# The normalisers of a wave attention, moved from a block of their own into the sampling block

## What is computed

```python
wp = silu(x @ w_wave + b_wave).reshape(b, l, 3, H)
freq_avg  = (sigmoid(wp[:, :, 0]) * 15 + 1).mean(-1)
phase_avg = (tanh(wp[:, :, 1]) * 16).mean(-1)
decay_avg = (sigmoid(wp[:, :, 2]) * 9.5 + 0.5).mean(-1)
qk = einsum("blhd,d->blh", silu(x @ w_query + b_query).reshape(b, l, H, POS), key_weight)
sample_pos = centers + stride_grid * freq_avg + phase_avg        # stride_grid: -16 .. 16
valid = (sample_pos >= 0) & (sample_pos < l)
rel = abs(stride_grid) * freq_avg
env = exp(-rel / max(decay_avg, 0.1))
attn = softmax(where(valid, qk * rel * SCALE, -inf)) * env * valid
attn = attn / (attn.sum(-1) + 1e-8)
out = einsum("blhsd,blhs->blhd", x[sample_pos], attn)            # then gates, w_out, the rest
```

## Time and profile before

| | us |
|---|---|
| median of 3 runs | 1732.34 (1732.11 to 1733.88) |
| the profiled execution's own time | 1732.2 |
| its span | 1730.5 |
| busy: TensorE, VectorE, ScalarE, GpSimd | 1529.6, 1361.0, 1016.0, 189.7 |
| mean granted TensorE clock, of full | 0.958 |

### The profile page before, as it was taken

How to read it: one execution, slowest core, us unless ns; L and a number is a source line. 1 busy time by engine, 2 the same in 40 slices (tenths; PEclk the granted TensorE clock), 3 DMA queues, 4 the chain that set the end, 5 groups by cost and what they waited for, 6 DMA issues and landing times. The chain is left out here.

```text
span 1730.5 us, 32390 instructions
## 1 busy us (share of the span) xinstructions
PE 1529.6 (88%) x9990; PEld 833.1 (48%) x9990; DVE 1361.0 (79%) x2955; ACT 1016.0 (59%) x1734; POOL 189.7 (11%) x366
## 2 busy tenths in 40 slices
PE   6028999996998999999999999999999876999997
PEld 5025565554655323322333233333322675999997
DVE  4879999963677888888888888888884575777774
ACT  3159999962544677767777677767777442222221
POOL 0021211103111000000000000000000271222222
PEclk9569999997999999999999999999999987999999
DMA  3030101002685522221222122221211467565561
GB/s 103 0 86 13 42 20 42 20 25 85 218 247 202 140 59 69 68 63 51 61 68 68 48 53 68 67 63 53 58 44 44 133 228 272 207 212 202 201 202 55
DMA packets 159151, 171.30 MB, mean 99 GB/s; under 512 B 73102, under 2 KB 119183, under 8 KB 158992
## 3 DMA queue, kind: packets, MB, share of 16 engines
q1 hardware_dynamic: 153008, 155.54, 29.7%
q0 software_dynamic: 4432, 12.66, 1.9%
q10 hardware_dynamic: 1552, 1.30, 0.2%
HBM read 120.73 MB, written 49.23 MB: 98 GB/s over the span
## 5 line engine op out<-in xcount | busy, mean ns | idle before, releaser
L1386 DVE TENSOR_REDUCE at_mx<-at_pmx 128x1 f32<-128x512 f32 x980 | 620.0, 681 | 61.9 <-PE at_pmx L1452 60.9
L1373 ACT ACTIVATE at_p<-at_pst 128x512 f32<-128x512 f32 x1024 | 539.3, 601 | 218.9 <-PE at_pst L1471 207.9
L1452 PE MATMUL at_pmx<-at_k,at_q 96*128 96x512 bf16 x980 | 375.3, 383 | 1.0 <-DVE at_mx L1386 0.7
L1471 PE MATMUL at_pst<-at_q,at_k 99*128 99x512 bf16 x1024 | 351.9, 381 | 14.6 <-ACT at_p L1373 12.2
L1481 PE MATMUL at_pacc<-at_p,at_v 128*32 128x512 f32 x2048 | 272.8, 604 | 0.9 <-ACT at_p L1373 0.7
L1452 PEld LDWEIGHTS at_pmx<-at_k,at_q 96*128 96x128 bf16 x980 | 95.0, 97 | 237.2 <-DVE at_mx L1386 175.6
L539 ACT ACTIVATE ws_A<-ws_steps,par_beta,par_alpha 128x672 f32<-128x672 bf16 (+2 forms) x256 | 200.2, 856 | 4.8 <-issue 4.2
L629 DVE TENSOR_TENSOR ws_AT<-ws_pA,ws_hitT 128x768 f32<-128x768 f32 (+1 forms) x192 | 180.1, 950 | 16.4 <-PE ws_pA L688 15.4
L1471 PEld LDWEIGHTS at_pst<-at_q,at_k 99*128 99x128 bf16 x1024 | 99.2, 98 | 161.4 <-ACT at_p L1373 98.4
L688 PE MATMUL ws_pA<-ident,ws_A 128*128 128x128 f32 x1088 | 146.6, 280 | 25.9 <-ACT ws_A L539 24.5
L2011 DVE STREAM_TRANSPOSE ex_zr<-ex_row 32x64 f32<-32x64 f32 x608 | 143.2, 236 | 21.4 <-DMA ex_row<-scratch_routed 13.6
(11 more groups left out here) (243 smaller groups left out, 1464.0 us busy)
## 6 DMA issues: line engine op xcount, KB each, us to landing
ex_w<-in_L_ffn_w SPq DMA_DIRECT2D x39, 1024.0 KB, 5.1
at_q<-scratch_qs SPq DMA_DIRECT2D x192, 64.0 KB, 2.7
at_k<-scratch_ks SPq DMA_DIRECT2D x192, 64.0 KB, 2.8
ex_row<-scratch_routed SPq DMA_DIRECT2D x39, 258.0 KB, 4.9
scratch_v<-gp_v SPq DMA_DIRECT2D x8, 1024.0 KB, 7.8
at_v<-scratch_v SPq DMA_DIRECT2D x32, 256.0 KB, 3.3
w<-in_L_ffn_w SPq DMA_DIRECT2D x16, 512.0 KB, 4.2
scratch_qs<-gp_split SPq DMA_DIRECT2D x16, 384.0 KB, 3.1
```

What stands on the lines that cost most here:

```text
L1373: a.activation(pt[k // 2 % 4][:, k % 2, :], pst[bank(k)][:], ACT.Exp).then_inc(exped, 1)
L1386: v.reduce_max(mx[u % 2][:, m // 2, m % 2:m % 2 + 1], pmx[bank(m)][:], AX.X).then_inc(red, 1)
L1452: nc.tensor.matmul(pmx[bank(m)][:], qst[u][0:ROWS, h, nt * P:(nt + 1) * P], kst[u][0:ROWS, h, kh * HALF:(kh + 1) * HALF], start=True, stop ...
L1471: nc.tensor.matmul(pst[bank(k)][:], kst[u][:, h, t * P:(t + 1) * P], qst[u][:, h, p * HALF:(p + 1) * HALF], start=True, stop=True).then_in ...
```

## The change

The normalisers' block goes. `tanhs` and `qk` now lie in the memory of `ws_A`, which is free until the first weights, and so does a new table `spread`: it has a column for each of 64 lanes (head and tile) and each distance k from 1 to 16, and as a matmul's moving side it gives the lane's slope times k minus the lane's top. GpSimd makes it, and the iotas, in the projection block. VectorE starts the sampling block with the short chain, with counts in bf16 and 100 for 1000 as the far constant. The arguments come from TensorE: it turns slopes and tops (four groups of 64 lanes) and multiplies them with `spread`, 2 x 512 columns a group. ScalarE takes the exponentials from PSUM in four groups, with distance 0 apart. VectorE forms `share` = (env + 1e-8) x count once and weighs each group with it (min with 1, then multiply), written with the distance outermost; TensorE sums the 17 distances of a group by matmuls with the identity. Between the groups stand the first unit's tile chains. The scratch memory is that of `ws_AT`. Parts that only rename are left out of the diff.

```diff
+WINDOWS = 17 * P + 4 * 2 * 16
...
-            wave_parameters(nc, sem, sb, ps, io, dr, ident, par)
-            wave_sampling(nc, sem, sb, ps, io, dr, ident, identb, par, gate_loads, gates_in)
+            weights = sb(wave, "ws_A", [P, WH // 2, WINDOWS])
+            grid = Grid(lambda *a: sb(wave, *a), weights)
+            with ExitStack() as ctx:
+                project_waves(nc, sem, lambda *a: sb(ctx, *a), lambda *a: ps(ctx, *a), io, ident, par["lpos"], grid)
+            wave_sampling(nc, sem, sb, ps, io, dr, ident, identb, par, weights, grid, gate_loads, gates_in)
...
+class Grid:
+    NK = REACH + 1
+    FAR = 100
+    def __init__(self, sb, weights):
+        words = weights[:].rearrange("p h n -> p (h n)")
+        self.steps = sb("grid_steps", [P, STEPS])
+        self.ks = sb("grid_ks", [P, self.NK], BF16)
+        self.far = sb("grid_far", [P, self.NK], BF16)
+        self.spread = words[:, 0:1024].rearrange("p (n k) -> p n k", k=REACH)
+        self.tanhs = words[:, 1024:1792].rearrange("p (t n h) -> p t n h", n=3, h=WH)
+        self.qk = words[:, 1792:2048].rearrange("p (t h) -> p t h", h=WH)
...
+        @block.gpsimd
+        def _(pool):
+            g = nc.gpsimd
+            near = ident[:, 0:2 * TILES].unsqueeze(2).to_broadcast([P, 2 * TILES, REACH])
+            away = ident[:, 2 * TILES:P].unsqueeze(2).to_broadcast([P, 2 * TILES, REACH])
+            g.iota(grid.spread, pattern=[[0, 2 * TILES], [1, REACH]], base=1, channel_multiplier=0,
+                   allow_small_or_imprecise_dtypes=True).then_inc(made, 1)
+            g.iota(lpos[:], pattern=[[0, B], [P, BT]], base=0, channel_multiplier=1,
+                   allow_small_or_imprecise_dtypes=True)
+            g.iota(grid.steps[:], pattern=[[1, STEPS]], base=-REACH, channel_multiplier=0,
+                   allow_small_or_imprecise_dtypes=True)
+            g.iota(grid.ks[:], pattern=[[1, grid.NK]], base=0, channel_multiplier=0,
+                   allow_small_or_imprecise_dtypes=True)
+            g.iota(grid.far[:], pattern=[[-1, grid.NK]], base=grid.FAR, channel_multiplier=0,
+                   allow_small_or_imprecise_dtypes=True)
+            pool.wait_ge(made, 1)
+            g.tensor_tensor(grid.spread, grid.spread, near, ALU.mult).then_inc(made, 1)
+            pool.wait_ge(made, 2)
+            g.tensor_tensor(grid.spread, grid.spread, away, ALU.subtract).then_inc(made, 1)
...
-def wave_normalisers(nc, sem, sb, par, tanhs, qk, dr):
...
-        A = sb(ctx, "ws_A", [P, QUAD, WTOT])
...
+        NK, LANES, GROUPS = Grid.NK, WH * TILES, 4
+        GL = LANES // GROUPS
+        hold = [t[:].rearrange("p s l -> p (s l)") for t in AT]
+        P_ = hold[0][:, 0:LANES * NK].rearrange("p (n k) -> p n k", k=NK)
+        X = hold[0][:, LANES * NK:2 * LANES * NK].rearrange("p (k n) -> p k n", k=NK)
+        amT = hold[0][:, 2 * LANES * NK:2 * LANES * NK + GROUPS * P]
+        place_at = [0]
+        def part(n):
+            place_at[0] += n
+            return hold[1][:, place_at[0] - n:place_at[0]]
+        spot, spot2 = (part(TILES * STEPS).rearrange("p (t s) -> p t s", s=STEPS) for _ in range(2))
+        inside = part(TILES * STEPS).bitcast(BF16)[:, 0:TILES * STEPS].rearrange("p (t s) -> p t s", s=STEPS)
+        cnt, any_, tk, tk2 = (part(TILES * NK).bitcast(BF16)[:, 0:TILES * NK].rearrange("p (t k) -> p t k", k=NK) for _ in range(4))
+        reach, env, share = (part(TILES * NK).rearrange("p (t k) -> p t k", k=NK) for _ in range(3))
+        am = part(2 * LANES).rearrange("p (g w n) -> p g w n", g=GROUPS, w=2)
+        slope, top = (am[:, :, w, :].rearrange("p g (h t) -> p g h t", t=TILES) for w in range(2))
+        m2, lnD = (part(LANES).rearrange("p (g h t) -> p g h t", g=GROUPS, t=TILES) for _ in range(2))
+        mean = part(3 * TILES).rearrange("p (t n) -> p t n", n=3)
+        dec, gain, pitch = (part(TILES) for _ in range(3))
+        nd, ranges, powers, sums = (sem("wn_" + n) for n in ("dve", "ranges", "powers", "sums"))
+        LOCATED, RANGED, SPACED, NORMAL = 1, 2, 3, 4 + GROUPS
+        NEAREST, DECAYED, COPIED, LOGGED = 1, 2, 3, 4 + GROUPS
+        TURNED, SUMMED = 1, 2 + GROUPS
...
+                def normal_exps(j):
+                    a.wait_ge(sums, argued(j))
+                    nc.scalar.activation(P_[:, j * GL:(j + 1) * GL, 1:NK],
+                                         pA[j % RING][:].rearrange("p (n k) -> p n k", k=REACH), ACT.Exp).then_inc(powers, 1)
                 PLACE, LOCATE = (1, 3, 4, 6), (0, 0, 2, 3)
                 a.wait_ge(rows_made, 3)
-                for r in range(G):
-                    if r:
-                        place(0, 0, r - 1)
-                    locate(0, 0, r)
-                place(0, 0, G - 1)
+                a.wait_ge(ranges, LOCATED)
+                locate(0, 0, 0)
+                a.wait_ge(ranges, RANGED)
+                nc.scalar.activation(P_[:, :, 0].rearrange("p (g n) -> p g n", g=GROUPS), am[:, :, 1, :], ACT.Exp, scale=-1.0).then_inc(powers, 1)
+                a.wait_ge(ranges, SPACED)
+                nc.scalar.activation(env, reach, ACT.Exp, scale=-1.0).then_inc(powers, 1)
+                a.wait_ge(sums, TURNED)
+                nc.scalar.copy(amT, acc[0][:]).then_inc(powers, 1)
+                place(0, 0, 0)
+                locate(0, 0, 1)
+                normal_exps(0)
+                place(0, 0, 1)
+                locate(0, 0, 2)
+                normal_exps(1)
+                place(0, 0, 2)
+                locate(0, 0, 3)
+                normal_exps(2)
+                place(0, 0, 3)
+                normal_exps(3)
+                a.wait_ge(sums, SUMMED)
+                nc.scalar.activation(lnD, acc[1][:, 0:LANES].rearrange("p (g h t) -> p g h t", g=GROUPS, t=TILES), ACT.Ln).then_inc(powers, 1)
+                a.wait_ge(ranges, NORMAL)
...
-                for i in range(APART * G + LATER):
-                    for r in range(G):
-                        steps(0, 0, r, i - APART * r)
+                def first_steps(start, stop):
+                    for i in range(start, stop):
+                        for r in range(G):
+                            steps(0, 0, r, i - APART * r)
+                def over(a, n):
+                    return a.unsqueeze(2).to_broadcast([P, TILES, n])
+                def heads(a):
+                    return a.unsqueeze(1).unsqueeze(1).to_broadcast([P, GROUPS, WH // GROUPS, TILES])
+                def lanes(a):
+                    return a.rearrange("p t (g h) -> p g h t", g=GROUPS)
+                def along(a):
+                    return a[:].unsqueeze(1).to_broadcast([P, TILES, NK])
+                def weigh(j):
+                    dve.wait_ge(powers, exped(j))
+                    v.scalar_tensor_tensor(out=X[:, :, j * GL:(j + 1) * GL].rearrange("p k (h t) -> p h t k", t=TILES),
+                                           in0=P_[:, j * GL:(j + 1) * GL, :].rearrange("p (h t) k -> p h t k", t=TILES),
+                                           scalar=1.0, in1=share.unsqueeze(1).to_broadcast([P, GL // TILES, TILES, NK]),
+                                           op0=ALU.min, op1=ALU.mult).then_inc(ranges, 1)
+                freq, phase, invf, mid, kmin, kmax, lpos = (par[n][:] for n in ("freq", "phase", "invf", "mid", "kmin", "kmax", "lpos"))
+                c = Chain(dve, nd)
+                c.link(v.reduce_sum(mean, grid.tanhs, AX.X))
+                c.did(v.tensor_scalar(freq, mean[:, :, 0], 7.5 / WH, 8.5, ALU.mult, ALU.add))
+                c.did(v.tensor_scalar(phase, mean[:, :, 1], 16.0 / WH, None, ALU.mult))
+                c.link(v.tensor_scalar(dec, mean[:, :, 2], 4.75 / WH, 5.25, ALU.mult, ALU.add))
+                c.did(v.tensor_tensor(mid, lpos, phase, ALU.add))
+                c.did(v.tensor_scalar(dec, dec, 0.1, None, ALU.max))
+                c.link(v.reciprocal(invf, freq))
+                c.did(v.tensor_scalar(mid, mid, -1.0, 0.5, ALU.mult, ALU.add))
+                c.did(v.tensor_scalar(pitch, freq, float(POS) ** -0.5, None, ALU.mult))
+                c.link(v.reciprocal(gain, dec))
+                v.tensor_tensor(mid, mid, invf, ALU.mult).then_inc(ranges, 1)
+                c.did(v.tensor_tensor(gain, gain, freq, ALU.mult))
+                c.link(v.tensor_tensor(spot, grid.steps[:].unsqueeze(1).to_broadcast([P, TILES, STEPS]), over(freq, STEPS), ALU.mult))
+                c.link(v.tensor_tensor(spot2, spot, over(lpos, STEPS), ALU.add))
+                c.link(v.tensor_tensor(spot, spot2, over(phase, STEPS), ALU.add))
+                c.link(v.tensor_scalar(spot2, spot, float(L), None, ALU.is_lt))
+                c.link(v.scalar_tensor_tensor(out=inside, in0=spot, scalar=0.0, in1=spot2, op0=ALU.is_ge, op1=ALU.mult))
+                c.did(v.tensor_copy(cnt[:, :, 0], inside[:, :, REACH]))
+                c.link(v.tensor_tensor(cnt[:, :, 1:NK], inside[:, :, REACH + 1:STEPS], inside[:, :, REACH - 1::-1], ALU.add))
```

(75 more changed lines are left out.)

91 lines of the change are left out of this document (removed).

## The result

The changed kernel takes 1712.41 us, the median of 4 runs (1711.22 to 1714.5); the kernel before, beside it on the same chip, 1733.11 (1732.11 to 1736.92). The ratio is 0.9878, 95% interval 0.9859 to 0.9897: faster, by 20.7 us where the forecast had 28.5. The measured 1712.41 lies 2.9 us above the upper end of the range given.

What follows compares the result with a forecast made beforehand. The prediction took VectorE's chain to carry the time to the first weight exponentials: 112.53 to 84.0, 28.5 us earlier, carried unchanged to the end, so 1732.2 - 28.5 = 1703.7 us, range 1700.5 to 1709.5.

Steps and rivals of the forecast that it cites:

- E: Start of the first `ws_A` weight exponentials in the sampling stage: forecast at 84.0 us, against 112.53 before the change.
- (5): Last group's sums, logarithm, beta and exponential table load, one after another: 4.2 us in all, 1.84 for the seventeen matmuls.
- the carry of the shift to the end: From the first weight exponentials on, both programs do the same in order, so the 28.5 us shift reaches the end unchanged.
- (1): Sampling block's start: GpSimd's added work in the projection block costs nothing; VectorE starts at 44.81, 1.18 us later than before.
- (2): Two big memsets beside VectorE's short ops stretch them; the 1056-wide chain starts at 50.2, bounds 47.5 and 51.2.
- (3): VectorE's narrow work: 5.94 us for the 1056-wide chain, 5.46 for counts and tops; tops ready at 61.6.
- (4): VectorE's tile steps, `share`, four weighing ops of 1.29 us and one 2.0 us wait: 17.5 us, to 79.8.
- scattered write: Rival: weighing writes with 1 KB gaps take 2.3 us each, plus TensorE at half clock and no counts gain: 1709.4; 12%.
- the sums become the bound: Rival: TensorE's 68 accumulating matmuls, p us each, set the first exponentials: 1712.0 at p = 0.28, 4%; 1744.0 at 0.75, 2%.
- Cheaper still: Rival: table load before its waits (1.28 us), counts 0.8 shorter, spot chain from 49.4: 1700.8; 6%.
- The drain of about 1.38 us: Trainium skill's rule for ScalarE table switches, not adopted in the forecast; by it the time would be 1.4 us higher.

Runs made afterwards that it cites:

- Late memsets: Against the changed kernel, GpSimd clears the x edge buffers only after VectorE's short chain has located the mean position; 1716.57 us, ratio 0.9878 to the kernel before.
- contiguous terms: Against the changed kernel, the weighed product is written with the distance innermost, so TensorE reads with a step of 17 words; 1719.31 us, ratio 0.9893 to before.
- the split: Against the changed kernel, contiguous f32 terms, TensorE sums groups 0 and 1 together, then group 2, VectorE sums group 3; 1706.96 us, ratio 0.984 to before.

## Why the prediction was wrong in size

The direction held, and E carried the time; what bounds E did not: the prediction built it along VectorE's chain, and TensorE's sums ended last. Of the 7.5 us between forecast and profiled time (1703.7, 1711.2), 4.2 are in E and 3.3 behind it. Either alone would have left the time inside the range, at 1707.9 or 1707.0. Step (5) below is the one whose reasoning failed; the carry of the shift to the end had no term at all.

(1) *Block start.* VectorE at 44.85, said 44.81. Right.

(2) *Memsets.* The reduction was not held and two tensor_scalars were, each to the end of a memset, as the Trainium skill has it (SBUF — State Buffer, "Who interferes with whom"). The 1056-wide chain started at 49.24, not 50.2: behind the first held op three more got through before the second hold. Late memsets start it 1.67 sooner in the same block; I had 2.7 between the value and the lower bound.

(3) *Narrow work.* 11.06 us to the tops at 60.30, said 11.4. The bf16 counts gained more than I took: a 544-wide tensor-tensor 0.46 in place of 0.73.

(4) *Interleaved stretch.* From `reach` to the last weighing 20.7 us, said 17.5: 3.1 of it is the weighing, 2.05 to 2.08 four times for 1.29. That was the first half of the rival "scattered write". It didn't set the end (contiguous terms). (1056 elements in 1.26 are 1.19 ns an element, not the 1.08 that the rival's counterargument gives; the 1.29 came from that row all the same.) VectorE's waits were 1.67 and 0.96, said 2.0 in one. The arguments took 9.26 us, said 7.6.

(5) *The last group is serial: the step that failed.* "Seventeen 64-column matmuls: 0.108 each" was taken from one record per matmul. An f32 matmul has two records here, and 17 of them take 3.82, not 1.84. The four groups, 15.3 us, no longer fit beside VectorE's 10.4 from the second weighing's start; they run on behind it for 4.9 us. The row was there: 32 records of L218 in 4.30 us are 16 matmuls of the code, 0.27 each, and I read them as 0.134. The same halving was in the arguments (eight matmuls, 0.48 each by my reading; 16 records of 0.43 at full clock). A bf16 transpose and an f32 transpose have one record each, which is why rows of transposes priced the sum at half.

The rival *the sums become the bound* named the mechanism and the formula: E = 71 + 68p + 2.3. With the measured p = 0.225 it gives 88.6, measured 88.24. I gave it 4% because the wrong reading of L218 spoke against it. That its 1712.0 (for p = 0.28) is so near the measured 1712.41 is luck: its E was 92.3, and what E did not lose the gate stage did. *Cheaper still* held in one part: the table load began with beta (86.94 and 86.96), so only 0.66 of its 1.28 lay behind it, and the last step took 1.74 in place of 2.3. The drain of about 1.38 us that the Trainium skill adds to each switch of tables (ScalarE: Activation LUTs, "What ACT_TABLE_LOAD costs") isn't in this trace either, neither ahead of the load (logarithm to 86.92, load at 86.94) nor behind it (load to 88.22, activation at 88.24).

The assumption that the shift of E is carried to the end was wrong by 3.3 us: 28.5 − 4.2 is 24.3, the span moved 21.0. 2.8 of it is the gate stage's wait and clock. The prediction said that both programs do the same from E on in the same order; they did, and 3.3 us were lost all the same.

## What to carry to other kernels

Divide a group's count in the trace by the matmuls of the code before you take a price from it; f32 matmuls had two records here, transposes and bf16 one. When work is moved to an idle engine, sum its time against the cover as for the engine that is relieved: here half of it there and half left behind gave the earliest E (36.72 after S), though the time did not tell it from the split. Carry a shift through every stage that waits on loads: here a wait grown from 1.01 to 2.34 us also cost the clock.
